# Softmax squares through DRAM, four long value matmuls, and outputs spread over the steps of a cross-attention kernel

## What is computed

```python
q = heads(x @ to_q_w)                    # 32 batches, 20 heads, 512 x 32
k = heads(ctx @ to_k_w); v = heads(ctx @ to_v_w)      # 77 tokens
p = softmax(q @ k.T / sqrt(32), axis=-1)              # 512 x 77 a head
out = merge(p @ v) @ to_out_w + to_out_b + x
```

## Time and profile before

| | |
|---|---|
| median of 3 runs | 2291.25 us (2284.69 to 2298.54) |
| the profiled execution, its own time | 2294.51 us |
| its span | 2292.6 us |
| mean granted TensorE clock | 0.931 |

### The profile page before, as it was taken

How to read it: one execution, slowest core, us unless ns; L and a number is a source line. 1 busy time by engine, 2 the same in 40 slices (tenths; PEclk the granted TensorE clock), 3 DMA queues, 4 the chain that set the end, 5 groups by cost and what they waited for, 6 DMA issues and landing times.

```text
span 2292.6 us, 71224 instructions
## 1 busy us (share of the span) xinstructions
PE 2091.9 (91%) x25840; PEld 1849.0 (81%) x25840; DVE 1183.8 (52%) x2772; ACT 1139.8 (50%) x5757; POOL 904.5 (39%) x1030
## 2 busy tenths in 40 slices
PE   8999977989898999989898989899999989898998
PEld 8999966878787877878787878787877878787887
DVE  4211115656565655656565656565655656565663
ACT  4211125655564555555454555554555555454553
POOL 1111134444444444434443444444444434443442
PEclk9999988999999998989898989998998989898999
DMA  7422133333333332333333323333332333333321
GB/s 256 135 101 97 67 77 68 92 92 91 92 91 91 84 89 71 91 87 91 85 91 81 91 60 91 92 91 91 85 88 72 91 87 91 85 91 82 89 63 42
DMA packets 180802, 206.80 MB, mean 90 GB/s; under 512 B 61952, under 2 KB 127568, under 8 KB 180400
## 3 DMA queue, kind: packets, MB, share of 16 engines
q1 hardware_dynamic: 174592, 182.69, 29.9%
q0 software_dynamic: 5808, 18.93, 2.3%
HBM read 140.67 MB, written 60.87 MB: 88 GB/s over the span
## 4 chain that ended last, share of the span: by engine, by line
issue 47%; POOL 31%; PE 6%; ACT 1%; POOLq 1%; DVE 0%; DMA 0%; ACTq 0%
POOL probs L593 17%; POOL x_t L588 7%; POOL x_bias L583 6%; PE p_bank L787 2%; PE p_bank L742 2%; ACT probs L618 1%; PE p_four L756 1%; PE p_four L775 1%; POOLq L592 1%; POOLq L587 0%; DMA bias_all<-in_L_xattn_to_out_b 0%; DVE q_t L681 0%; DVE negmax L660 0%; DVE turned L676 0%; POOLq L471 0%
## 5 line engine op out<-in xcount | busy, mean ns | idle before, releaser
L618 ACT ACTIVATE probs<-p_four,negmax 128x77 f32<-128x77 f32 x2560 | 787.9, 362 | 406.2 <-DVE negmax L660 406.2
L593 POOL TENSOR_TENSOR probs<-probs,rsum 128x308 f32<-128x308 f32 x640 | 447.1, 700 | 967.5 <-DVE rsum L666 965.2
L742 PE MATMUL p_bank<-x_t,wq_split 128*128 128x512 f32 x2400 | 673.5, 427 | 27.9 <-DVE q_t L681 18.1
L618 ACT ACTIVATION_READ_ACCUMULATOR probs<-p_four,negmax 128x1 f32 x2560 | 624.5, 244 | 0.0
L742 PEld LDWEIGHTS p_bank<-x_t,wq_split 128*128 128x128 f32 x2400 | 472.8, 205 | 153.1 <-DVE q_t L681 36.3
L787 PE MATMUL p_bank<-wo_split,o_t 128*128 128x320 f32 x3840 | 593.8, 310 | 0.0
L787 PEld LDWEIGHTS p_bank<-wo_split,o_t 128*128 128x128 f32 x3840 | 574.1, 188 | 14.6 <-issue 6.5
L660 DVE TENSOR_REDUCE negmax<-p_four 128x4 f32<-128x308 f32 x640 | 284.4, 479 | 240.2 <-PE p_four L756 239.4
L775 PE MATMUL p_four<-turned,v_sb 32*32 32x128 f32 (+1 forms) x15360 | 257.6, 297 | 158.3 <-ACT probs L618 86.0
L676 DVE STREAM_TRANSPOSE turned<-probs 128x384 f32<-128x384 f32 x640 | 359.4, 562 | 64.0 <-POOL probs L593 63.8
L775 PEld LDWEIGHTS p_four<-turned,v_sb 32*32 32x32 f32 (+1 forms) x15360 | 190.1, 107 | 220.6 <-issue 205.3
(11 more groups left out here) (31 smaller groups left out, 777.6 us busy)
## 6 DMA issues: line engine op xcount, KB each, us to landing
x_raw<-in_x SPq DMA_DIRECT2D x128, 320.0 KB, 5.2
x_bias<-in_x SPq DMA_DIRECT2D x32, 1280.0 KB, 6.0
out<-x_bias SPq DMA_DIRECT2D x128, 320.0 KB, 2.9
v_sb<-v_scratch SPq DMA_DIRECT2D x128, 160.0 KB
k_diag<-k_scratch SPq DMA_DIRECT2D x640, 19.2 KB, 1.7
k_scratch<-k_out POOLq DMA_DIRECT2D x45, 256.0 KB, 2.6
ctx_raw<-in_ctx SPq DMA_DIRECT2D x19, 512.0 KB, 4.6
v_scratch<-v_out POOLq DMA_DIRECT2D x38, 160.0 KB, 2.1
```

The costliest lines, as they stand in the source:

```text
L593: nc.gpsimd.tensor_tensor(heads_of(t), heads_of(t), rsum[:, slot, t, :].unsqueeze(2).to_broadcast([P, HG, N_TXT]), ALU.mult).then_inc(prob ...
L618: last = nc.scalar.activation(heads_of(t)[:, h, :], s_bank[t][:, h * N_TXT:(h + 1) * N_TXT], ACT.Exp, bias=negmax[:, slot, t, h:h + 1], ac ...
L742: last = nc.tensor.matmul(q_bank[:, :], wq_s[:, w, c, g * P:(g + 1) * P], x_t[:, a, c, :], start=c == 0 and i == 0, stop=c == CC - 1 and i ...
```

## The change

The value product gets its operand in another layout, by way of DRAM. Once the four tiles of a group are transposed in squares, SyncE writes `turned` (128 partitions x 3 blocks x 512, 768 KB) to `p_scratch` by one DMA. When the value product of the group before has read `probs_t`, three DMAs read it back with the keys on 77 partitions and all 512 queries of a head along them (616 KB). So the value product of a head is one matmul: 77 rows, 32 columns of weights, 512 columns moving; four make a group. The values are loaded once, 77 rows for each group, by five DMAs a batch in place of eight. There is one `probs_t` and two `turned`.

The value product has a PSUM bank of its own, and the waits on the score banks go. The order strings change: TensorE begins each step with the scores, then the value product of the group two before, then the queries, and then outputs. The eight halves of output are spread 1, 2, 2, 1, 2 over the steps of the batch after, so that the last one (P7) falls into the batch after that. VectorE takes reciprocal and transpose of a tile right behind each other, with the value copy between the first and second tile. On ScalarE the value copy comes between the second and third tile's exponentials, and all five X pieces stand in step 3; GpSimd has its five X pieces in step 3 too, and the bias additions in steps 4 and 0.

The diff, cut to its core (passing of `p_scratch`, semaphore names and the renamed argument `age` are left out):

```diff
-TENSOR = orders("V Q0 Q1 S0 S1 S2 S3 Q2 Q3 Q4",
-                "V Q0 Q1 S0 S1 S2 S3 Q2 Q3 Q4 O0 O1",
-                "V Q0 Q1 S0 S1 S2 S3 Q2 Q3 Q4 O2 O3",
-                "V Q0 Q1 S0 S1 S2 S3 Q2 Q3 Q4 O4 O5",
-                "V O6 S0 S1 S2 S3 O7 Q0 Q1 Q2 Q3 Q4")
-SCALAR = orders("V S0 S1 S2 S3 Q",
-                "V S0 S1 S2 S3 Q",
-                "V S0 S1 S2 S3 Q",
-                "V S0 S1 S2 S3 Q X0 X1 X2",
-                "V X3 X4 S0 S1 S2 S3 Q")
-VECTOR = orders("V M0 M1 M2 M3 R0 R1 T0 R2 T1 R3 T2 T3 Q",
-                "V M0 M1 M2 M3 R0 R1 T0 R2 T1 R3 T2 T3 Q Y0 Y1 O0 O1",
-                "V M0 M1 M2 M3 R0 R1 T0 R2 T1 R3 T2 T3 Q Y2 Y3 O2 O3",
-                "V M0 M1 M2 M3 Y4 R0 R1 T0 R2 T1 R3 T2 T3 Q O4 O5",
-                "V M0 M1 M2 M3 O6 R0 R1 T0 R2 T1 R3 T2 T3 O7 Q")
-POOL = orders("N0 N1 N2 N3",
-              "N0 N1 N2 N3 B0",
-              "N0 N1 N2 N3 B1 B2",
-              "N0 N1 N2 N3 B3 X0 X1 X2",
-              "X3 X4 N0 N1 N2 N3")
+TENSOR = orders("S0 S1 S2 S3 V Q0 Q1 Q2 Q3 Q4 P7",
+                "S0 S1 S2 S3 V Q0 Q1 Q2 Q3 Q4 O0 O1",
+                "S0 S1 S2 S3 V Q0 Q1 Q2 Q3 Q4 O2 O3",
+                "S0 S1 S2 S3 V Q0 Q1 Q2 Q3 Q4 O4",
+                "S0 S1 S2 S3 V O5 Q0 Q1 Q2 Q3 Q4 O6")
+SCALAR = orders("S0 S1 V S2 S3 Q",
+                "S0 S1 V S2 S3 Q",
+                "S0 S1 V S2 S3 Q",
+                "S0 S1 V S2 S3 Q X0 X1 X2 X3 X4",
+                "S0 S1 V S2 S3 Q")
+VECTOR = orders("M0 M1 M2 M3 R0 T0 V R1 T1 R2 T2 Q R3 T3 P7",
+                "M0 M1 M2 M3 R0 T0 V R1 T1 R2 T2 Q R3 T3 Y0 O0 Y1 O1",
+                "M0 M1 M2 M3 R0 T0 V R1 T1 R2 T2 Q R3 T3 Y2 O2 Y3 O3",
+                "M0 M1 M2 M3 R0 T0 V R1 T1 R2 T2 Q R3 T3 Y4 O4",
+                "M0 M1 M2 M3 R0 T0 V R1 T1 O5 R2 T2 R3 T3 Q O6")
+POOL = orders("N0 N1 N2 N3 C2 C3",
+              "N0 N1 N2 N3",
+              "N0 N1 N2 N3",
+              "N0 N1 N2 N3 X0 X1 X2 X3 X4",
+              "N0 N1 N2 N3 B0 B1")
...
+    p_scratch = nc.dram_tensor("p_scratch", (2, KB, P, HG * P), F32, kind="Internal").ap()
...
-        v_sb = [sbuf(f"v_sb{i}", [P, KB, C]) for i in range(2)]
+        v_sb = sbuf("v_sb", [N_TXT, CC, P])
...
+        probs_t = sbuf("probs_t", [N_TXT, P // SQ, HG, P])
...
-        bank = [stack.enter_context(nc.psum_tensor(f"p2_bank{i}", [P, 512], F32)) for i in range(3)]
-        four = stack.enter_context(nc.psum_tensor("p2_four", [P, QT, 512], F32))
-        s_bank, pv_bank = [four[:, t, :] for t in range(QT)], four[:, :, 512 - P:512]
-        q_bank, fill_bank = bank[0], bank[1:3]
+        bank = [stack.enter_context(nc.psum_tensor(f"p2_bank{i}", [P, 512], F32)) for i in range(8)]
+        s_bank, q_bank, pv_bank, fill_bank = bank[0:4], bank[4], bank[5], bank[6:8]
...
+            def load_v(b, g):
+                sp.dma_start(v_sb[:, g, :], v_scratch[bass.ds(b * N_TXT, N_TXT), g * P:(g + 1) * P])\
+                  .then_inc(v_loaded[g], DMA)
...
+            def write_probs(n, slot):
+                sp.wait_ge(probs_turned, QT * (n + 1))
+                sp.dma_start(p_scratch[slot].rearrange("k p c -> p k c"),
+                             turned[slot][:, :, :, :, :].rearrange("p k h t q -> p k (h t q)"))\
+                  .then_inc(probs_written[slot], DMA)
+
+            def read_probs(n, slot):
+                sp.wait_ge(probs_written[slot], DMA // 2 * (n - slot) + DMA)
+                for k in range(KB):
+                    rows = min(SQ, N_TXT - k * SQ)
+                    sp.dma_start(probs_t[k * SQ:k * SQ + rows, :, :, :].rearrange("p i h c -> p i (h c)"),
+                                 p_scratch[slot, k].rearrange("(i p) c -> p i c", p=SQ)[0:rows])\
+                      .then_inc(probs_read[slot], DMA)
...
+            def body(b, parity, age, last):
                 for g in range(CC):
+                    n, slot = CC * b + g, (parity + g) % 2
+                    if not (age == 0 and g < 2):
+                        sp.wait_ge(pv_done, n - 1)
+                        if g < 2:
+                            load_v(b, g + CC - 2)
+                        elif not last:
+                            load_v(b + 1, g - 2)
+                    if not (age == 0 and g == 0):
+                        read_probs(n - 1, 1 - slot)
+                    for kind, k in TENSOR[(g - 1) % CC]:
+                        if kind == "O" and k % 2 == 1 and g > 0 and age > 0:
+                            store_out(b - 1, 1 - parity, k // 2)
+                        if kind == "O" and k % 2 == 1 and g == 0 and age > 1 or kind == "P" and age > 1:
+                            store_out(b - 2, parity, k // 2)
                     if not last:
                         sp.wait_ge(s_done, TILES * b + QT * (g + 1))
                         load_k(b + 1, g)
-                    if g == 1:
+                    if g == 2:
                         load_x_bias(b, parity)
                     if g == 4 and not (isinstance(b, int) and b + 2 >= B):
                         load_x(b + 2)
+                    write_probs(n, slot)
...
-                    dve.wait_ge(pv_done, n - 1)
+                    dve.wait_ge(probs_written[slot], DMA // 2 * (n - slot))
...
-                if t == 0 and not (isinstance(b, int) and CC * b + g < 2):
-                    pe.wait_ge(ot_ready, CC * b + g - 1)
...
-            def sum_values(b, g, slot, parity, last=False):
+            def sum_values(b, g, slot):
...
-                pe.wait_ge(probs_turned, QT * (n + 1))
-                if not last:
-                    pe.wait_ge(exp_done, TILES * b + QT * (g + 2))
...
+                pe.wait_ge(probs_read[slot], DMA * KB // 2 * (n - slot) + DMA * KB)
+                for h in range(HG):
+                    last = nc.tensor.matmul(pv_bank[h * HD:(h + 1) * HD, :], v_sb[:, g, h * HD:(h + 1) * HD],
+                                            probs_t[:, :, h, :], start=True, stop=True)
+                last.then_inc(pv_done, 1)
```

More of the change, by code:

```diff
@@ L395, in _, with attend @@
             blocks(pe, body)
-def attend(nc, x_v, x_rows, bias, out, kept, k_scratch, v_scratch, x_loaded):
+def attend(nc, x_v, x_rows, bias, out, kept, k_scratch, v_scratch, p_scratch, x_loaded):
     with ExitStack() as stack:
@@ L433, in attend @@
         probs_zero, probs_turned, pv_done = sem("probs_zero"), sem("probs_turned"), sem("pv_done")
-        values_clear = sem("values_clear")
+        probs_written = [sem(f"probs_written{i}") for i in range(2)]
+        probs_read = [sem(f"probs_read{i}") for i in range(2)]
         q_done, q_high, q_ready = sem("q_done"), sem("q_high"), sem("q_ready")
@@ L468, in batches, with steps @@
         def batches(eng, body):
-            body(0, 0, True, False)
-            with eng.Fori(0, (B - 2) // 2) as i:
+            body(0, 0, 0, False)
+            body(1, 1, 1, False)
+            with eng.Fori(0, (B - 4) // 2) as i:
                 for half in range(2):
-                    body(2 * i + (1 + half), (1 + half) % 2, False, False)
-            body(B - 1, (B - 1) % 2, False, True)
-        def steps(order, b, parity, first, last):
+                    body(2 * i + (2 + half), half, 2, False)
+            body(B - 2, 0, 2, False)
+            body(B - 1, 1, 2, True)
+        def steps(order, b, parity, age, last):
             for g in range(CC):
                 for kind, k in order[g]:
-                    left_out = (kind == "O" and first or kind in "XY" and last
-                                or kind == "V" and first and g < 2
+                    left_out = (kind in "OC" and age == 0 or kind == "P" and age < 2 or kind in "XY" and last
+                                or kind == "V" and age == 0 and g < 2
                                 or kind == "Q" and last and g == CC - 1)
@@ L556, in body @@
                         load_x(b + 2)
-                if not first:
-                    store_out(b - 1, 1 - parity, QT - 1)
-            body(0, 0, True, False)
-            with sp.Fori(0, (B - 4) // 2) as i:
-                for half in range(2):
-                    body(2 * i + (1 + half), (1 + half) % 2, False, False)
-            for b in (B - 3, B - 2, B - 1):
-                body(b, b % 2, False, b == B - 1)
+                    write_probs(n, slot)
+            batches(sp, body)
+            store_out(B - 2, (B - 2) % 2, 2)
+            sp.wait_ge(pv_done, CC * B - 1)
+            read_probs(CC * B - 1, (CC * B - 1) % 2)
+            store_out(B - 2, (B - 2) % 2, 3)
             for t in range(QT):
@@ L598, in _, with body @@
                 xt_low_part(0, c)
-            def body(b, parity, first, last):
-                for g, slot, kind, k in steps(POOL, b, parity, first, last):
+            def body(b, parity, age, last):
+                for g, slot, kind, k in steps(POOL, b, parity, age, last):
                     if kind == "N":
@@ L609, in _ @@
             batches(pool, body)
+            for t in (2, 3):
+                add_bias(B - 1, (B - 1) % 2, t)
         @block.scalar
```

(12 more changed lines are left out.)

77 lines of the change are left out of this document (23 added, 54 removed).

## The result

The changed kernel takes 2163.07 us (median of 4 runs, 2151.74 to 2168.56) where the kernel before takes 2287.97 (4 runs beside it, 2282.91 to 2298.54): a ratio of 0.944, 95% interval 0.939 to 0.949. The profiled execution took 2162.03 us with a span of 2160.2.

What follows compares the result with a forecast made beforehand. VectorE's order was taken as the bound: 55 us a batch, plus 2.5 for the branch stall and 2.3 for the clock, 59.8 against 60.8; over 31 batches, plus 9 at the end, span 2271, forecast 2270, range 2190 to 2345.

Steps and rivals of the forecast that it cites:

- TensorE's work, value product: TensorE: a value product of 1.1 us, four heads side by side, and 49.9 us of warm work a batch.
- The rival of heads in turn: Value product: the four heads run one behind the other, 3.8 us each time, 2463 us in all; chance 0.08.
- VectorE's order becomes the bound, 55 us a batch: VectorE: each transpose waits for GpSimd's normalisation of the same tile; 9.07 us a step, 55 us a batch with delays.
- The branch stall stays: VectorE's loop branch: its 5.3 us stall remains and its chain carries it, 5 us a pair, 2.5 a batch.
- The rival without the stall: VectorE has no stall at the branch, or less waiting: 57.3 us a batch, 2193 us; chance 0.15.
- The clock: TensorE, step 0: 3.9 us of idling brings one 6.8 us stretch at 1.2 GHz every batch, costing 2.3 us.
- The round trip hidden: DRAM write 4.4 us and reads 4.6, 9.0 in all, hidden with 1 to 2 us to spare, costing nothing.
- End: After the last transpose: write, read, value product and copies, then outputs at the slow clock, some 9 us later.
- Head and batch 0 "stay": Kernel's start and first batch: time unchanged, batch 0 at 52.7 us without outputs.
- would join: SyncE's loop branch: grown from 74 transfers a pair to 108, it would stall too, inside the round trip.

Runs made afterwards that it cites:

- The reordering alone: Changed kernel with VectorE taking each reciprocal one tile ahead of its transpose: 2113.26 us, ratio 0.924.
- the trip was taken away too: Changed kernel with VectorE's reciprocals a tile ahead and no DRAM write or reads, softmax left out of the output: 1979.10 us, ratio 0.863.
- the shift by 20 instructions: Kernel before with 20 tiny memsets at the start of VectorE's program, ahead of its loop: 2285.89 us, ratio 0.997.
- the stop put back: Changed kernel with four reductions of a constant tile at the end of VectorE's loop body, once in two batches: 2226.32 us, ratio 0.972.
- the run without it: Changed kernel without the DRAM write and reads, the value product reading a tile filled once: 2168.14 us, ratio 0.945.
- a third of the value product: Kernel before with the value product of the first block of 32 keys alone, other keys left out: 2213.83 us, ratio 0.965.
- the loads are reordered: Changed kernel with x loads in two pairs in step 0, x_bias behind the write: 2169.66 us; with VectorE's reciprocals also a tile ahead, 1991.99 us.

## Why the prediction was wrong

The direction was right and the size was not. By its steps:

- **TensorE's work, value product.** Right: 1.00 us against 1.1, 49.93 us busy against 49.9, the four heads side by side. The rival of heads in turn falls. The 1.2 us estimated from the Trainium skill's figure (TensorE: Matmul & The Clock Gate, Measured speedup vs the span model) stood a little above too.
- **VectorE's order becomes the bound, 55 us a batch.** Right: 55.0 in the undisturbed batches, the pattern R, wait, T as described, GpSimd's block 2.7 us late for step 4 against 2.6, scores waiting 3.5 for the query against 3.9, and 1.1 against 1.8. The reordering alone bears it out with 50 us, and shows how near the next limit stood: the batch fell from 56.5 to 55.0 only, until the trip was taken away too (50.9).
- **"The branch stall stays".** This is the step that failed. It was 2.5 us a batch, 77 us in all; the trace has none. "VectorE's loop body keeps its work, so I keep its 5.3 us" was the error: the shift by 20 instructions showed that the same body can stop or not. The rival without the stall had it, at a chance of 0.15 and 2193 us. The term was also priced too high: the stop put back cost 4.5 us for 6.4, so 5.3 would have cost an estimated 3.7 a pass (5.3 x 4.5 / 6.4) and not 5.0; and it was counted for 31 batches, 15.5 pairs, where the loop of the changed kernel goes back 13 times. That makes an estimated 48 us (3.7 x 13) rather than 77.
- **The clock.** Mis-sized: 2.3 us a batch forecast, for every batch; 1.5 measured (56.49 - 55.0). A slow stretch costs 2.5 or 3.3 us when it comes (57.5 or 58.3 less 55.0), but it comes in about half of the batches. What went wrong is the step "3.9 us of idling is more than the 2.5 that dropped the clock before, so each batch has one stretch": a wait of 3.54 us at 951.05 was followed by a granted clock of 1.00, and one of 2.74 at 1005.99 by 0.67.
- **The round trip hidden.** Right in the body, as the run without it shows, with the write at 3.6 us where 4.4 was taken.
- **End.** The trip did cost 9.0 us there: the last transpose ends near 2127.0 and the last value product starts at 2136.04. But the last batch ahead of it was shorter too, so the end from batch 31's first scores is 82.5 us against 81.6, one more and not the forecast eight (nine for the trip less the one that a batch gains): 7 us.
- **Head and batch 0 "stay".** They did not: batch 1's first scores start at 382.9 us where they started at 387.6, 5 us earlier. The forecast had put this at nothing.

Over the thirty batches from batch 1 to batch 31, 3.3 us a batch are missing (59.8 - 56.5): 2.5 x 30 = 75 us for the stop and 0.8 x 30 = 24 for the clock. With 5 at the head and 7 at the end that is 111 us, and the forecast span of 2271 stands 111 above the measured 2160.

Where did the gain of 125 us come from? Not directly from the work that TensorE lost, an estimated 2.4 us a batch (52.3 - 49.9), since TensorE now waits for VectorE. The batch lost its alternation (the stops of TensorE and VectorE are absent, ScalarE's lies behind a wait); TensorE's stop went with the shorter program of the value product. By the two batches of the earlier trace rows that is an estimated 6.7 us a pair or 3.4 a batch of the 4.3, and 0.9 is left for the exchange of the two chains: TensorE's order with its waits for exponentials before, VectorE's with its waits for GpSimd after. This split is arithmetic and no run shows it: the new operand with the old order strings, and the new orders with the old operand, were not run.

What stays open: why VectorE's loop lies well in every version of the changed kernel here and badly in the one before, why SyncE's lies badly in two of them, and why ScalarE's stop reaches the chain in some versions and not in others. ScalarE stops at its branch in every run here, for 2.3 to 6.8 us. That TensorE's stop belongs to the size of its program is supported, not settled: it is absent in the changed kernel and with a third of the value product (15600 matmuls in place of 25840), but the packets fetched fell in the second case only from 230 to 150. The Trainium skill (Advanced Engine Details and Errata, ISA Cache) gives TensorE 128 KB and a line 16 KB or 256 instructions, which makes an estimated eight lines. By the windows a pass holds 1470 matmuls and 1470 weight loads before (estimated 11.5 lines), 832 and 831 with the third (6.5), and 590 and 590 in the changed kernel (4.6). So the stop is there above eight lines and absent below, as that rule would have it; but some nine packets a pass are still fetched with the third ((150 - 25) / 14), which the rule alone does not explain. For the other engines that section gives two lines and says nothing of placement, and placement is what decided for VectorE. SyncE, which by that rule "would join" in the changed kernel, passes its branch in 0.3 us there, and stops 4.2 us only once the loads are reordered.

## What to carry to other kernels

A stop at a loop's branch can come and go with where the program lies, so it must not be carried over as a term from one build to the next. Give it a case of its own, look at every engine's first instruction behind the branch before crediting one, and compare the packets of the instruction queues. Limits lie behind one another: a moved load was worth nothing or 121 us depending on whether VectorE's wait had gone first, so repeat a measurement of an edit after each bound that falls. A transfer on the critical path wants a quiet moment: here four loads of small rows in two pairs around it, in place of four together, were worth 87 us (2079 to 1992).

## What the runs showed of the hardware

- Twenty one-column fills ahead of the loop removed a stop of 5.3 us at VectorE's branch and 69 packets on q14 (172 to 103); another order of SyncE's loads, with 283 recorded instructions a pass in place of 284, brought one of 4.2 us and 65 packets (89 to 154). Three engines can stop at one branch at once (TensorE 5.8, VectorE 5.3, ScalarE 5.0 us).
- The same wait of TensorE for the query, 3.53 us at 1063.49, 3.54 at 951.05 and 2.74 at 1005.99, was followed by 10.4 us at a granted clock of 0.58, 1.00 and 0.67.
- A write of 768 KB landed in 3.6 us (the median in the changed kernel), in up to 8.9 us right behind four x loads of 320 KB in 640-byte packets, and in up to 9.8 behind one x_bias load of 1280 KB. Moving the x loads to GpSimd's queue left TensorE's wait for the data at 2.7 us.
